# First expert stage of a two-layer transformer kernel: tiles of one expert taken in pairs, with a split first product of 256 columns

## The reference, cut to what matters

```python
logits = jnp.einsum('btd,ed->bte', x, router_w)
top_vals, top_idx = jax.lax.top_k(logits, K)
top_w = jax.nn.softmax(top_vals, axis=-1)
h = jnp.einsum('nd,edh->enh', xf, w1)
h = jnp.square(jax.nn.relu(h))
y = jnp.einsum('enh,ehd->end', h, w2)
out = sum over the 2 chosen experts of weight * y
```

## Time and profile before

| what | value |
|---|---|
| median of 3 runs | 766.41 us (765.76 to 768.55) |
| the profiled execution's own time | 768.04 us |
| its span, first to last instruction | 766.3 us |
| share of the span busy: TensorE, VectorE, ScalarE, GpSimd | 95%, 74%, 52%, 60% |
| TensorE, 250 to 280 us (in the expert stage) | busy 30.00 of 30.00 us, granted clock 1.00 |

### The profile page before, as it was taken

The page is one execution under the profiler, slowest core; times in us unless marked ns, Lnnn a source line. Parts: engine busy times, 40 slices in busy tenths (PEclk is TensorE's granted clock), DMA queues, the critical chain, the costliest instruction groups (busy, mean ns, idle before and its releaser), DMA issues.

```text
span 766.3 us, 19644 instructions
## 1 busy us (share of the span) xinstructions
PE 731.5 (95%) x6336; PEld 651.7 (85%) x6336; DVE 569.2 (74%) x1265; ACT 398.1 (52%) x873; POOL 458.3 (60%) x577
## 2 busy tenths in 40 slices
PE   6999999999999999999998999899999899999994
PEld 4888864999999999999986999777778678888883
DVE  4887864778988887988648887589898766766642
ACT  5444534544454444545524888556677665444511
POOL 3677777999877876887422223024377545665363
PEclk9999999999999999999999999889999999999998
DMA  9799642345444435433248986135548855666352
GB/s 262 210 269 281 202 139 79 84 139 145 121 124 122 118 103 138 127 111 110 66 136 265 328 280 212 31 78 126 118 81 187 256 194 130 149 146 150 52 56 27
DMA packets 151105, 113.99 MB, mean 149 GB/s; under 512 B 59359, under 2 KB 141282, under 8 KB 151012
## 3 DMA queue, kind: packets, MB, share of 16 engines
q1 hardware_dynamic: 137812, 86.94, 40.9%
q0 software_dynamic: 12624, 25.35, 13.2%
q10 hardware_dynamic: 576, 0.53, 0.3%
HBM read 68.68 MB, written 40.80 MB: 143 GB/s over the span
## 4 chain that ended last, share of the span: by engine, by line
PE 89%; DVE 4%; issue 2%; ACT 2%; DMA 1%; POOL 1%; SPq 0%; POOLq 0%; ACTq 0%; DVEq 0%
PE bank L864 17%; PE banks L882 13%; PE bank L1135 11%; PE banks L1146 5%; PE bank L935 5%; PE banks L738 4%; PE banks L803 4%; PE bank L745 3%; PE bank L1042 3%; PE bank L1025 3%; PE banks L792 3%; PE banks L952 3%; PE bank L1014 2%; PE bank L851 2%; PE banks L999 1%
## 5 line engine op out<-in xcount | busy, mean ns | idle before, releaser
L864 PE MATMUL bank<-rw,rt 128*128 128x128 f32 x1136 | 138.5, 275 | 0.6 <-ACT rw L1240 0.6
L864 PEld LDWEIGHTS bank<-rw,rt 128*128 128x128 f32 x1136 | 132.5, 192 | 1.3 <-issue 1.3
L882 PE MATMUL banks<-r_split,rt_split 128*128 x852 | 118.7, 289 | 0.1
L2135 POOL DMA_INDIRECT ults_by_choice_and_token<-rw,y_id x71 | 81.3, 1145 | 51.2 <-ACT rw L1298 43.3
L1688 DVE TENSOR_TENSOR rw<-rw 128x512 f32<-128x512 f32 x71 | 69.7, 982 | 53.8 <-ACT rw L1285 53.3
L882 PEld LDWEIGHTS banks<-r_split,rt_split 128*128 128x128 f32 x852 | 106.1, 190 | 0.3 <-issue 0.3
L1135 PE MATMUL bank<-r_split 128*128 128x512 f32 x384 | 89.6, 391 | 1.3 <-issue 1.1
L1291 ACT ACTIVATE rt_split<-rw 128x512 fp32r<-128x512 f32 x71 | 44.8, 631 | 82.4 <-DVE rw L1688 78.3
L1135 PEld LDWEIGHTS bank<-r_split 128*128 128x128 f32 x384 | 71.4, 188 | 16.3 <-issue 1.9
L2234 POOL DMA_INDIRECT out_x<-r,idx x32 | 50.2, 1569 | 53.1 <-DVE r L1993 45.4
L2104 POOL DMA_INDIRECT rows_by_expert<-rw,slots x64 | 69.8, 1091 | 18.6 <-issue 9.7
(11 more groups left out here) (253 smaller groups left out, 1565.9 us busy)
## 6 DMA issues: line engine op xcount, KB each, us to landing
rt<-in_w SPq DMA_DIRECT2D x24, 512.0 KB, 4.8
rw<-rows_by_expert SPq DMA_DIRECT2D x71, 128.0 KB
r<-in_w SPq DMA_DIRECT2D x16, 512.0 KB, 6.9
rt<-ults_by_choice_and_token SPq DMA_DIRECT2D x32, 256.0 KB, 3.9
rw<-in_x SPq DMA_DIRECT2D x16, 256.0 KB, 4.7
rw<-in_sin_q SPq DMA_DIRECT2D x32, 128.0 KB
rw<-x_layer SPq DMA_DIRECT2D x16, 256.0 KB
x_plus_bias<-rw SPq DMA_DIRECT2D x16, 256.0 KB, 3.2
```

The costliest lines, as they stand in the source:

```text
L864: last = pe.matmul(bank[1 + t % 2][:, k * P:(k + 1) * P], c_w1[:, t % 2, c, k * P:(k + 1) * P], c_xT[:, t % 2, c, :], start=c == 0, stop=c ...
L882: last = pe.matmul(bank[6 + t % 2][:, 0:D], h[:, t % XB, c, :], w[:, ds(e2, 1), o + c * D:o + (c + 1) * D], start=n == 0, stop=n == 3 * HC ...
L2135: pool.indirect_dma_start(y0_d[:, :], bass.IndirectOffsetOnAxis(y_id[:, t:t + 1].bitcast(I32), 0), c_y[:, t % XB, :], None, bounds_check=l ...
```

## The change

The first 56 tiles (T1 = 2 * ND) become 28 pairs; each pair is two tiles of one expert. The table puts the experts' full pairs first and what is left behind them, 15 single tiles. The single tiles go as before, one place on in each loop.

For a pair, TensorE makes 4 transposes into one bank. ScalarE takes the high part of the 512 columns (`high_rows_T`), VectorE the low part (`low_rows_T`). The copy of w1 goes; ScalarE rounds w1 to a high part in two halves (`high_w1`), VectorE subtracts to get the low part in two halves (`low_w1`); there is one buffer for each, and both are made once for a pair. TensorE runs 24 matmuls of fp32r with 256 columns (`hidden_pair`): first the hidden blocks 0 and 1 of both tiles into bank 1, then 2 and 3 into bank 2. So "relu 2d" and "square 2d" are now half the hidden units of both tiles. VectorE squares the first of the two, ScalarE the second (`square_odd`), except in the first pair. The results are made tile by tile as before, both of pair d-1 behind the hidden values of pair d, and both wait for both halves. The loads wait for the transposes of the pair that holds tile t-4. `add_attention` moves to the step of the next pair. SyncE's own loop stays as it is but for that wait. The transposes of pair 1 now stand ahead of the first hidden values. The split of the third stage's weights moves to step 60 on ScalarE and step 62 on VectorE, since its room holds the pairs' rows till then.

The diff, cut:

```diff
--- before.py
+++ after.py
...
-        XB = 4
+        XB, ND = 4, 28
+        T1 = 2 * ND
+        NTR = ST0 - ND
...
+        c_xhi = [wq1_hi[:, b, 0:2 * D].rearrange("p (c n) -> p c n", c=DC) for b in range(2)]
+        c_xlo = [rws[:, XB * D:XB * D + 2 * D].rearrange("p (c n) -> p c n", c=DC), wq1_hi[:, :, 2 * D:3 * D]]
+        c_w1hi, c_w1lo = (rts[:, k * DC * H:(k + 1) * DC * H].rearrange("p (c n) -> p c n", c=DC) for k in range(2))
...
+        def group(t):
+            return t // 2 if t < T1 else t - ND
...
-                    sp.wait_ge(cT_ps, t - XB + 1)
+                    sp.wait_ge(cT_ps, group(t - XB) + 1)
...
-            def transpose_rows(t):
-                pe.wait_ge(xg_in[t % XB], 32 * (t // XB + 1))
-                if t == 0:
+            def transpose_rows(g):
+                tiles = (2 * g, 2 * g + 1) if g < ND else (g + ND,)
+                for t in tiles:
+                    pe.wait_ge(xg_in[t % XB], 32 * (t // XB + 1))
+                if g == 0:
                     pe.wait_ge(kvm_r, NB)
-                if t == 1:
+                if g == 1:
                     pe.wait_ge(q_sb, 2 * NQ)
-                if t >= 2:
-                    pe.wait_ge(cT_sb, t - 1)
+                if g >= 2:
+                    pe.wait_ge(cT_sb, g - 1)
+                    pe.wait_ge(xlo_d, min(g - 1, ND))
+                n = len(tiles)
                 for c in range(DC):
-                    last = pe.transpose(bank[TB[t % 2]][:, c * P:(c + 1) * P], c_xg[:, t % XB, c * P:(c + 1) * P],
-                                        ident[:, :])
+                    for i, t in enumerate(tiles):
+                        last = pe.transpose(bank[TB[g % 2]][:, (n * c + i) * P:(n * c + i + 1) * P],
+                                            c_xg[:, t % XB, c * P:(c + 1) * P], ident[:, :])
                 last.then_inc(cT_ps, 1)
 
+            def hidden_pair(d):
+                if d == 0:
+                    pe.wait_ge(m_sb, NB)
+                pe.wait_ge(w1_r, DC * (d + 1))
+                pe.wait_ge(xlo_d, d + 1)
+                for b in range(2):
+                    if d >= 1:
+                        pe.wait_ge(relu_sb, 2 * d + b - 1)
+                    for k in range(2):
+                        n = 0
+                        o = (2 * b + k) * P
+                        for c in range(DC):
+                            for w, x in ((c_w1hi, c_xhi), (c_w1hi, c_xlo), (c_w1lo, c_xhi)):
+                                last = pe.matmul(bank[1 + b][:, k * 2 * P:(k + 1) * 2 * P], w[:, c, o:o + P],
+                                                 x[d % 2][:, c, :], start=n == 0, stop=n == 3 * DC - 1)
+                                n += 1
+                    last.then_inc(hT_ps, 1)
...
+                done = t | 1 if t < T1 else t
+                pe.wait_ge(hi_r, done + 1)
+                pe.wait_ge(lo_c, done + 1)
...
+            for d in range(ND):
+                transpose_rows(d + 1)
+                hidden_pair(d)
+                if d >= 1:
+                    result0(2 * d - 2)
+                    result0(2 * d - 1)
+                for i in range(NE):
+                    if o_step[i] in (2 * d + 1, 2 * d + 2):
+                        attend(i)
+            for t in range(T1, ST0 + 2):
+                if t + 1 < ST0:
+                    transpose_rows(group(t + 1))
                 if t < ST0:
-                    transpose_rows(t)
-                if 2 <= t < ST0 + 1:
-                    hidden0(t - 1)
-                if t >= 3:
-                    result0(t - 3)
-                for i in range(NE):
-                    if o_step[i] == t:
-                        attend(i)
+                    hidden0(t)
+                result0(t - 2)
...
+            def high_rows_T(d):
+                act.wait_ge(cT_ps, d + 1)
+                if d >= 2:
+                    act.wait_ge(hT_ps, 2 * d - 2)
+                act.activation(c_xhi[d % 2], bank[TB[d % 2]][:, :].rearrange("p (c n) -> p c n", c=DC), ACT.Copy)\
+                   .then_inc(cT_sb, 1)
+
+            def high_w1(d):
+                if d == 0:
+                    act.wait_ge(table_r, 4)
+                    act.wait_ge(m_ps, NB)
+                    act.wait_ge(w1_in, 16 * (2 + E))
+                e1 = act.value_load(tile_e[0:1, 2 * d:2 * d + 1], min_val=0, max_val=E - 1)
+                if d >= 1:
+                    act.wait_ge(hT_ps, 2 * d)
+                for c in range(DC):
+                    act.activation(c_w1hi[:, c, :].unsqueeze(1), r1[:, ds(e1, 1), c * H:(c + 1) * H], ACT.Copy)\
+                       .then_inc(whi_r, 1)
...
+                    high_rows_T(0)
+                    high_w1(0)
...
+            def square_odd(t):
+                act.wait_ge(relu_sb, t + 1)
+                act.wait_ge(lo_c, t - 1)
+                act.activation(c_sq[:, t % 2, :], c_r[:, t % 2, :], ACT.Square).then_inc(sq_r, 1)
...
+            for d in range(ND):
+                if d + 1 < ND:
+                    high_rows_T(d + 1)
+                else:
+                    copy_rows_T(T1)
+                if d >= 2:
+                    copy_y(2 * d - 4)
+                    copy_y(2 * d - 3)
+                relu0(2 * d)
+                if d + 1 < ND:
+                    high_w1(d + 1)
+                relu0(2 * d + 1)
+                act.wait_ge(sq_r, 2 * d + 1)
+                if d >= 1:
+                    square_odd(2 * d + 1)
+                high0(2 * d)
+                high0(2 * d + 1)
+            copy_y(T1 - 4)
+            for t in range(T1, ST0 + 3):
+                if t + 1 < ST0:
+                    copy_rows_T(t + 1)
+                copy_y(t - 3)
                 if t < ST0:
-                    copy_rows_T(t)
-                if t >= 4:
-                    copy_y(t - 4)
-                if t < ST0 + 1:
-                    relu0(t - 1)
-                    high0(t - 1)
-                if t == 20:
+                    relu0(t)
+                    high0(t)
+                if t == T1 + 4:
...
+            link(dve.tensor_copy(pair_n, n_i[:, 2 * E:3 * E]))
+            link(dve.tensor_scalar(pair_n, pair_n, 2.0, None, ALU.mult))
+            link(dve.tensor_tensor_scan(pair_incl, one8[:, :], pair_n, 0.0, ALU.mult, ALU.add))
+            link(dve.tensor_tensor(u2[:, 0:E], pair_n, pair_incl, ALU.subtract))
+            link(dve.tensor_scalar(u2[:, 0:E], u2[:, 0:E], float(T1), 0.0, ALU.add, ALU.max))
+            link(dve.tensor_tensor(u2[:, 0:E], u2[:, 0:E], pair_n, ALU.min))
+            link(dve.memset(u2[:, E:E + 1], 0.0))
+            link(dve.tensor_tensor(d_one, n_f, u2[:, 0:E], ALU.subtract))
+            link(dve.tensor_tensor_scan(s_incl, one8[:, :], d_one, float(T1), ALU.mult, ALU.add))
+            link(dve.tensor_tensor(d_one, u2[:, 1:E + 1], n_f, ALU.subtract))
+            link(dve.tensor_scalar(d_one, d_one, float(SPAN), None, ALU.add))
+            link(dve.tensor_scalar(d_pair, pair_n, -1.0, float(SPAN), ALU.mult, ALU.add))
+            for lo, hi, incl, d in ((0, T1, pair_incl, d_pair), (T1, ST0, s_incl, d_one)):
+                link(dve.tensor_tensor(past[:, :, lo:hi], over_mid(iota_t[:, lo:hi], E), over_last(incl, hi - lo), ALU.is_ge))
+                link(dve.tensor_tensor(past_d[:, :, lo:hi], past[:, :, lo:hi], over_last(d, hi - lo), ALU.mult))
...
+            def low_w1(d):
+                e1 = dve.value_load(tile_e[0:1, 2 * d:2 * d + 1], min_val=0, max_val=E - 1)
+                for c in range(DC):
+                    dve.wait_ge(whi_r, DC * d + c + 1)
+                    dve.tensor_tensor(c_w1lo[:, c, :].unsqueeze(1), r1[:, ds(e1, 1), c * H:(c + 1) * H],
+                                      c_w1hi[:, c, :].unsqueeze(1).bitcast(F32), ALU.subtract).then_inc(w1_r, 1)
+
+            def low_rows_T(d):
+                dve.wait_ge(cT_sb, d + 1)
+                dve.tensor_tensor(c_xlo[d % 2], bank[TB[d % 2]][:, :].rearrange("p (c n) -> p c n", c=DC),
+                                  c_xhi[d % 2].bitcast(F32), ALU.subtract).then_inc(xlo_d, 1)
...
+            dve.drain().then_inc(table_r, 1)
+            low_rows_T(0)
+            low_w1(0)
+            for d in range(ND):
+                if d + 1 < ND:
+                    low_rows_T(d + 1)
+                for i in range(NE):
+                    if o_step[i] in (2 * d - 1, 2 * d):
+                        add_attention(i)
+                square0(2 * d)
+                if d + 1 < ND:
+                    low_w1(d + 1)
+                else:
+                    copy_w1(T1)
+                    copy_w1(T1 + 1)
+                if d == 0:
+                    square0(1)
+                low0(2 * d)
+                low0(2 * d + 1)
+            for t in range(T1, ST0 + 1):
+                if T1 + 1 <= t < ST0 - 1:
+                    copy_w1(t + 1)
+                if t > T1:
+                    low0(t - 1)
                 if t < ST0:
-                    copy_w1(t)
-                low0(t - 2)
```

(8 more changed lines are left out.)

70 lines of the change are left out of this document (26 added, 44 removed).

## The result

The changed kernel takes 761.99 us (median of 9 runs, 758.18 to 763.92) against 768.21 of the kernel before on the same chip (9 runs): ratio 0.9919 [0.9898, 0.994]. The forecast was 755.6 us, 1.4% less than 766.41; 0.8% less came. The sign was right, the size was not.

What follows compares the result with a forecast made beforehand. TensorE, busy 95% of the span, was taken to bound the kernel. Its 20.7 us saved, less 1.5 for VectorE's low weights, 4.2 for the start and 4.2 for SyncE's queue, left 10.8: 755.6 us, range 748.5 to 766.

Steps and rivals of the forecast that it cites:

- TensorE's work: Expert stage: a pair falls from 6.88 to 6.14 us, saving 0.74 each, 20.7 us for 28 pairs.
- the two rows that bounded it: Spacing of a pair's 24 matmuls: 0.112 would save 3.9 us more in all, 0.120 would save 1.1 less.
- the weights' loop: Remaking the single-buffered weights between pairs: done by 5.2 to 5.6 us, wanted at 6.14, so cost zero, slack 0.5 to 0.9.
- the low hidden values: VectorE's input to a pair's results: ready at 7.8 us, results begin at 8.97, so cost zero, slack 1.1.
- My slower rival: `hidden_pair` waits for low weights held behind GpSimd, about 1.2 us a pair; 775 to 789 us, chance 0.13.
- the signs of being wrong: Pair period above 6.5 without attention, low-weight waits in most pairs, matmul above 0.125 us, row waits in over seven pairs.
- The start: Start of the expert stage: four losses sum to 4.8, less 0.6 there before, 4.2 us; bounds 2.5 to 7.
- the table: VectorE's tile table has 14 more small operations ahead of the last rotated keys; TensorE 0.4 us later with the wait.
- Tile 0 and the queries: Pair 0's transposes also need tile 1, 1.2 us; pair 1's transposes wait for ScalarE's last query copies, 1.3 us.
- Pair 1's weights: Between the first two pairs no results hide the remaking of weights: 2.35 less 0.44 of transposes, 1.9 us.
- SyncE's queue: Row loads queued behind stores waiting for VectorE's additions make pairs late: 4.2 us together, bounds 0 to 9.
- The seven odd steps: Steps with odd `o_step`, whose load belongs to a pair wanted soon; four cost nothing, two about 0.9 each, one 2.4.

Runs made afterwards that it cites:

- the kernel with the new first step: The four edits, plus pair 1's weight halves made around its rows in another order on ScalarE and VectorE; ratio to the kernel before 0.9846.
- the last kernel: The kernel with the new first step, with the loads of a pair's two tiles issued together, ahead of tables and stores; ratio to the kernel before 0.9894.
- stores later: Changed kernel with SyncE's queue storing the first 16 attention tiles, and loading x into their room, one step later; ratio to the kernel before 0.9904.
- first pair ahead: Changed kernel with pair 0's hidden values made ahead of pair 1's transposes on TensorE; 762.7 us, ratio to the kernel before 0.994.
- the four edits: Changed kernel with pair 0's hidden values first, last rotated keys ahead of the tile table, stores one step later, weights split by hidden units; ratio 0.9842.
- the keys moved: Changed kernel with the last rotated keys computed on VectorE ahead of the tile table instead of behind it; ratio to the kernel before 0.9952.
- weights by half: Changed kernel with w1 remade and waited for in halves by hidden units instead of halves by D; ratio to the kernel before 0.9901.
- stores and halves: Changed kernel with stores one step later in SyncE's queue and w1 split and waited for by halves of hidden units; ratio to the kernel before 0.9866.

## Why the prediction was right or wrong

**TensorE's work: right.** 20.7 us forecast, 261.5 - 240.9 = 20.6 came. The new form costs 0.118 here as in the third stage; the two rows that bounded it (0.112 and 0.120) were not needed. The 109 ns that I worked out from the 262 cycles of the Trainium skill (TensorE: Matmul & The Clock Gate, section Back-to-back issue gap) was not reached: the quickest of the 28 groups of 24 took 2.83 us, 0.118 each.

**VectorE's low weights: the step that failed.** The prediction has the weights' loop at "cost zero", with a slack of 0.5 to 0.9, and the low hidden values at "cost zero, slack 1.1"; for both together it allows 0.05 a pair, 1.5 us. Against a larger price it holds that "the means already hold such meetings". That is a wrong use of a mean. The subtraction's mean went from 0.93, in another place of the pair, to 1.149, and a wait is made by the long ones: 2.5 us, where the slack is 0.5. It cost 3.6 in later pairs, 1.55 at the step to the single tiles, and part of pair 1's 2.99. With GpSimd's rotation turned into writes 2.4 of the 3.6 and all of the 1.55 went; the rest of the 3.6 was no hold by GpSimd's reads, or not shown to be. The minimum, median and maximum of the same form stood in the trace before, 676/694/2470 ns for L1694, and the prediction used the mean alone. My slower rival named this mechanism at its right place, but as a hold by one operation of 1.04 us, and priced it at 1.2 us a pair in half of all pairs or in all. In fact a train of operations holds VectorE, and TensorE feels it hard a few times (1.2 at pair 15, 0.65 at pair 12) and lightly (0.1 to 0.2) in others. Rival and forecast each held a part. Of the signs of being wrong that the prediction names one came, once: a pair without attention took 7.30 us (236.45 to 243.75) where 6.5 was the limit.

**The start: 4.2 forecast, 6.2 measured** (stalls of 5.96, less the 0.6 that stood there, and 0.86 for the table). Tile 0 and the queries were near (2.5 against 2.47). Pair 1's weights took 2.99 for 1.9, since its second subtraction took 1.22 and started late; the first results' 0.50 I had at zero; the table was 0.86 for 0.4.

**SyncE's queue: right in size (3.7 for 4.2) by luck.** The seven odd steps stand for pairs 7, 11, 15, 18, 19, 22 and 23. I had priced 18 at 2.4, 11 and 19 at 0.9 each, and the rest at nothing. Waits came at 3, 5, 7, 9, 18 and 23: 0.6 at pair 18, none at 11 and 19, the longest (0.85 and a restart) at 23, and 1.9 of the 3.7 at pairs 3, 5 and 9, which I had not named. The early ones are tables waiting for GpSimd, a wait that I had counted for GpSimd's own sake and not as something in front of rows.

**The sum.** 10.8 forecast, 5.3 at the stage's end: 3.65 more for VectorE (3.6 + 1.55 - 1.5), 2.0 more for the start, 0.5 less for rows, 0.1 of TensorE's work, and 0.27 of lateness from before the change's place.

**From the stage to the total.** Of the stage's 5.3 us, the profiled spans keep 4.4 (766.3 to 761.9), the medians 6.2. Behind the stage the same program took 373.8 us before and 374.7 after. The cause is not settled. The dip of the granted clock described below does not explain it: both executions have one of the same size (0.84 at 480 to 500 us and 0.90 at 500 to 520 before, 0.74 and 1.00 after).

## What to carry to other kernels

A loop with half a microsecond of slack is not judged by means: take the longest durations of the form, ask what lies behind them (here trains of GpSimd operations that read SBUF beside VectorE's with two SBUF inputs), and price the loop with those. Slack is made by splitting what is waited for, not only by making engines faster: two halves of the weights took every later wait for them away while VectorE was held just as much. Look at the granted clock before calling a long group of matmuls a wait. At the start of a pipeline and in a queue shared by rows, tables and stores, removing one wait moves the next forward; count all inputs before pricing one.

## What the runs showed of the hardware

**VectorE behind GpSimd.** Numbers above: 2.5 us for an operation of 0.68, once 3.14 (L1792), with two SBUF inputs; 0.68 to 0.69 in 28 low rows with one input in PSUM, 8 of them beside GpSimd. The attention's additions, 0.41 with one input in PSUM, say less than the prediction took from them: in the kernel before only 3 of the 16 ran beside a tensor operation of GpSimd, in the changed one none. Where the rotation only writes SBUF, the subtraction's median is 0.69.

**The granted clock behind a wait.** In the kernel with the new first step, the clock fell to 0.51, the lower level of 1.2 GHz, from about 151.5 to 155, soon after TensorE had stood 1.25 us up to 143.65 and 1.83 us up to 150.06. Its columns are stretch and length, busy times of the engines (PE, PEld, DVE, ACT, POOL), clock, DMA share, GB/s:

```profile
146.00:150.00 4.00, 2.23 (x16) 1.77 (x14) 2.74 (x3) 0.44 (x1) 4.00 (x6) 1.00 0.30 82
...
151.50:155.00 3.50, 3.50 (x19) 3.50 (x18) 2.71 (x4) 1.60 (x4) 3.11 (x5) 0.51 0.45 130
155.00:157.00 2.00, 2.00 (x19) 2.00 (x18) 1.26 (x2) 1.90 (x4) 1.77 (x3) 1.00 0.43 131
```

19 matmuls in 3.5 us stand beside 19 in 2.0 right behind. The group of 24 took 4.42 instead of 2.87: 1.5 us, nearly as much as the wait itself. The same came behind the 2.84 in the last kernel.

The same came in five more runs, at pair 1, where TensorE had stood 2.3 to 2.8 us ahead of the hidden values: with writes only, stores later, first pair ahead, all squares on VectorE, and the four edits. There the 24 matmuls took 4.42 to 4.63 us. But in the changed kernel and in its repeat TensorE stood 2.7 us at the same place, and 2.4 with the keys moved, and the clock stayed at 1.00. So a wait of TensorE can cost 1.5 to 1.7 us beyond its own length, and its length alone does not say whether it will; what decides isn't shown. A stage that holds such a stretch is not to be compared with one that doesn't without taking it off.

**A dip that comes and goes.** At 480 to 500 us TensorE is idle for 3.7 us in the changed kernel, and the clock dips there or just behind, down to 0.50 for some 10 us in the changed kernel, in every profiled execution but one. The changed kernel, then the one with weights by half:

```profile
480.00:500.00 20.00, 16.27 (x266) 13.47 (x265) 13.93 (x47) 9.09 (x18) 1.60 (x4) 0.74 0.23 41
```

```profile
480.00:500.00 20.00, 16.96 (x334) 12.98 (x318) 18.61 (x68) 10.47 (x23) 3.75 (x7) 1.00 0.41 83
```

What follows the stage took 374.7 us in the first and 371.1 in the second, with the same program there. But the kernel with stores and halves has the dip too (0.74) and took 372.7, so how much of the 3.6 is the dip's isn't shown.
